# Attention stream cut into quarters, stages placed by quarter, layer norm applied on GpSimd

## The reference

```python
x = x + attn_a(layernorm(x))   # 16 heads share softmax(-|pos_i - pos_j| / 4), causal;
                               # pos = x @ w3d.T + b3d (3 numbers a token); values x @ wv.T + bv, then wo, bo
x = x + ffn(layernorm(x))      # sigmoid(xr @ W_r) * (relu(xk @ W_k)**2 @ W_v),
                               # xr, xk = mixtures of x and of x of the token before
x = x + attn_b(layernorm(x))   # 16 heads of 16: softmax(q.k / 4), causal, times v
x = x + ffn(layernorm(x))      # the same weights again
```

## Time and profile before

| | us |
|---|---|
| three runs | 2307.72, 2312.24, 2311.35 (median 2311.35) |
| profiled execution | 2312.75, span 2311.0, granted clock 0.888 |
| PE, DVE, ACT, POOL busy | 1933.2, 1502.9, 1234.3, 697.5 |
| first maximum of the stream | 195 us from the span's start |
| turns 1 to 7 end at | 452, 724, 1000, 1271, 1543, 1816, 2063 |

### The profile page before, as it was taken

The page is one execution under the profiler, slowest core; times in us unless marked ns, Lnnn a source line. Parts: engine busy times, 40 slices in busy tenths (PEclk is TensorE's granted clock), DMA queues, the critical chain, the costliest instruction groups (busy, mean ns, idle before and its releaser), DMA issues.

```text
span 2311.0 us, 32343 instructions
## 1 busy us (share of the span) xinstructions
PE 1933.2 (84%) x9842; PEld 977.6 (42%) x9842; DVE 1502.9 (65%) x4429; ACT 1234.3 (53%) x2673; POOL 697.5 (30%) x818
## 2 busy tenths in 40 slices
PE   5475888889888898888988888888988789898986
PEld 4343444444443444434444344434444344432433
DVE  3346677666676576766776567766767667787643
ACT  1632644755539454484546644485543945556563
POOL 2331242223323233233332233222332324322223
PEclk8787798979998899889998889988999889999998
DMA  3005013101231103211121112310122110231100
GB/s 96 0 31 106 1 29 83 19 10 29 65 83 28 28 7 87 56 29 28 38 83 28 29 29 65 83 29 1 29 74 73 29 28 20 71 67 29 29 20 19
DMA packets 64346, 97.26 MB, mean 42 GB/s; under 512 B 15655, under 2 KB 58029, under 8 KB 58030
## 3 DMA queue, kind: packets, MB, share of 16 engines
q1 hardware_dynamic: 64174, 95.20, 18.0%
HBM read 61.09 MB, written 33.55 MB: 41 GB/s over the span
## 4 chain that ended last, share of the span: by engine, by line
PE 62%; DVE 17%; ACT 10%; issue 7%; POOL 2%; DMA 1%; SPq 1%; DVEq 0%; POOLq 0%; ACTq 0%
PE o_bank L994 10%; PE max_bank L970 9%; PE side L879 9%; PE exp_bank L979 9%; PE side L835 6%; PE side L869 5%; PE side L921 4%; ACT pt L1030 4%; PE side L803 4%; DVE max_bank L1054 3%; ACT sq L479 3%; DVE st L243 3%; DVE xh L258 2%; PE side L815 2%; PE side L935 2%
## 5 line engine op out<-in xcount | busy, mean ns | idle before, releaser
L1030 ACT ACTIVATE pt<-exp_bank 128x512 f32<-128x512 f32 (+3 forms) x1536 | 685.9, 495 | 434.2 <-PE exp_bank L979 426.3
L1054 DVE CUSTOM_DVE_ANT_0 max_bank<-max_bank,mask 128x128 f32<-128x128 f32 (+3 forms) x1024 | 482.3, 514 | 221.6 <-PE max_bank L970 214.8
L979 PE MATMUL exp_bank<-qs,ks 98*128 98x512 bf16 (+3 forms) x1536 | 529.3, 355 | 68.0 <-ACT pt L1030 61.9
L970 PE MATMUL max_bank<-ks,qs 96*128 96x512 bf16 (+3 forms) x1536 | 528.8, 356 | 64.8 <-DVE piece_max L1054 38.9
L1058 DVE TENSOR_REDUCE piece_max<-max_bank 128x1 f32<-128x512 f32 x512 | 325.2, 684 | 93.5 <-PE max_bank L970 93.0
L994 PE MATMUL o_bank<-pt,v 128*17 128x512 f32 (+3 forms) x3072 | 356.7, 539 | 3.9 <-ACT ot L1040 2.3
L1106 POOL TENSOR_SCALAR_AFFINE_SELECT pt<-pt 128x512 f32<-128x512 f32 x256 | 174.9, 683 | 574.8 <-ACT pt L1030 574.6
L970 PEld LDWEIGHTS max_bank<-ks,qs 96*128 96x128 bf16 x1536 | 156.4, 103 | 366.9 <-DVE piece_max L1054 126.7
L979 PEld LDWEIGHTS exp_bank<-qs,ks 98*128 98x128 bf16 x1536 | 155.7, 102 | 292.2 <-ACT pt L1030 185.9
L803 PE MATMUL side<-ident,xh 128*128 128x128 f32 x512 | 109.3, 383 | 137.9 <-DVE xh L258 137.9
L458 ACT ACTIVATE xt<-side 128x512 f32<-128x512 f32 x128 | 74.6, 598 | 249.5 <-PE side L803 249.5
(11 more groups left out here) (93 smaller groups left out, 2231.8 us busy)
## 6 DMA issues: line engine op xcount, KB each, us to landing
parts_dram<-parts SPq DMA_DIRECT2D x64, 384.0 KB, 2.6
qs<-parts_dram SPq DMA_DIRECT2D x192, 128.0 KB, 6.5
ks<-parts_dram SPq DMA_DIRECT2D x32, 384.0 KB, 4.7
xs<-in_L_attn_a_x_dram SPq DMA_DIRECT2D x16, 512.0 KB, 4.5
ks<-parts_dram SPq DMA_DIRECT2D x32, 256.0 KB, 5.3
out_dram<-xs SPq DMA_DIRECT2D x16, 512.0 KB, 3.5
ks<-parts_dram SPq DMA_DIRECT2D x32, 128.0 KB, 5.7
qs<-neg_maxT SPq DMA_DIRECT2D x64, 8.0 KB, 1.8
```

The lines of the kernel that those rows point to most:

```text
L970: pe.matmul(max_bank[k % MAX_BANKS][:, 0:k1 - k0], qs[r][0:KROWS, j, P * tile:P * (tile + 1)], ks[r][0:KROWS, j, k0:k1], start=True, stop= ...
L979: pe.matmul(exp_bank[k % EXP_BANKS][:, 0:q1 - q0], ks[r][:, j, P * kt:P * (kt + 1)], qs[r][:, j, q0:q1], start=True, stop=True).then_inc(s ...
L1030: act.activation(pt[:, e % 2, j, 0:q1 - q0], exp_bank[k % EXP_BANKS][:, 0:q1 - q0], ACT.Exp, scale=SCALE).then_inc(exp_done, 1)
L1054: dve.tensor_tensor_reduce(max_bank[k % MAX_BANKS][:, 0:w], max_bank[k % MAX_BANKS][:, 0:w], mask[:, HALF - w:HALF], 1.0, LOWEST, ALU.add, ...
```

## The change

The tables `CHUNKS`, `TURNS` and `CHUNKS_AT` go. The unit of time is now a quarter, one head of a piece. `STAGES` gives each half of each stage a start in quarters, and `JOBS` gives every use of a side bank a line in its stage: name, number, first quarter, number of parts, quarters between them, quarters until the bank is emptied. `place` hands out the banks in order of use, puts each part of a job (two matmuls, or a set of transposes) into a quarter of its own, and moves a job to later when both banks are taken; `clock` moves the other engines' steps with them. In `schedule` every part is a generator that yields the quarter from which it may go on. The ffn's two halves start 16 quarters apart and overlap, `att1` of the next image starts inside `proj3`, and `ffn4` starts 32 quarters after `ffn2`. A full turn still has 192 quarters (48 pieces).

The layer norm is applied by POOL (`pool_normalise`), four instructions in quarters of their own, and the statistics have double buffers. The difference of neighbours goes to `xr` itself, `tm` no longer holds it. The stack for an image's first group is loaded at the end of `sp_proj3`. Nothing is added to or taken from the arithmetic.

```diff
-HALF_FFN = 11
-TAIL = 2 * (NS * (B - 1) + LEAD + (NG - 1) * NP + TPH + 3) + 1
-CHUNKS_AT = [0] * (2 * SLOTS)
...
+TURN = 4 * NS
+ATT1, FFN2, FFN4, PROJ3 = -44, 50, 82, 114
+FIRST = {("att1", 0): -220, ("ffn2", 0): -126, ("proj3", 0): -74,
+         ("att1", 1): -28, ("ffn2", 1): 66, ("proj3", 1): 114}
+OUTPUT_AT = [4 * (LEAD + TPH + 1) + 1, 4 * (LEAD + NP + 1) + 1]
+LN_HALF = {"att1": 8, "ffn2": 16, "ffn4": 16, "proj3": 12}
...
+PIECE_TIME = [2 + (q1 - q0) // P for _, q0, q1 in KEY_PIECES] + [5, 5, 5]
+PIECE_AT = [34 + sum(PIECE_TIME[:p]) for p in range(NP + 4)]
...
+JOBS = {"ln": [("tr", c, 12 + c, 1, 1, 2) for c in range(NC)],
+        "att1": [("values1", t, 16 + t + TPH * (t // TPH), 1, 1, 2) for t in range(NT)] +
+                [("positions", k, 29 + k, 1, 1, 1) for k in range(6)] +
+                [("attend", t, PIECE_AT[attended_from(t)] + 2, t // 2 + 1, 1, 2) for t in range(NT)],
+        "ffn": [("keys", j, 24 + 2 * j, 2, 1, 1) for j in range(2)] +
+               [("receptance", j, 31 + 2 * j, 2, 1, 1) for j in range(2)] +
+               [("products", j, 36 + 2 * j, 2, 1, 2) for j in range(2)],
+        "proj3": [("project", j, 24 + 3 * j, 2, 1, 1) for j in range(8)] +
+                 [("values3", j, 26 + 6 * j, 2, 3, 2) for j in range(4)]}
...
+    rows = [(4 * NP * (g + 1) + 1, ("maxima", g)) for g in range(GROUPS)]
+    rows += [(OUTPUT_AT[h] + 4 * NP * g + 5, ("output", g, h)) for g in range(GROUPS) for h in range(2)]
...
-            def apply(h):
-                q = q0 + h
-                dve.wait_ge(rstd_ready, q + 1)
-                if q > 0:
-                    dve.wait_ge(tr_full, 2 * q)
-                for t in range(TPH):
-                    last = dve.tensor_scalar(xh[:, t, :], src[:, TPH * h + t, :], mv[:, t, 0:1],
-                                             rstd[:, t:t + 1], ALU.subtract, ALU.mult)
-                last.then_inc(xh_ready, 1)
...
+        def pool_normalise(at, s, n, h):
+            pool, q = nc.gpsimd, LN_AT[s, n, h]
+            r, src = q % 2, xs[n % X_BUFFERS]
+            yield at(6)
+            pool.wait_ge(ln_step, 3 * q + 3)
+            pool.tensor_tensor(rstd[:, r, :], var_eps[:, r, :], minus_half[:, :], ALU.pow).then_inc(rstd_ready, 1)
+            pool.wait_ge(rstd_ready, q + 1)
+            if q > 0:
+                pool.wait_ge(tr_full, 2 * q)
+            for t in range(TPH):
+                yield at(7 + t)
+                pool.tensor_scalar(xh[:, t, :], src[:, TPH * h + t, :], mv[:, r, t, 0:1], rstd[:, r, t:t + 1],
+                                   ALU.subtract, ALU.mult).then_inc(xh_ready, 1)
...
-            for u in range(2 * SLOTS):
-                t, s = divmod(u, 2)
-                att(t, s)
-                rows(t, s)
-                for _ in range(CHUNKS_AT[u]):
-                    next(tail if u >= TAIL else chunks)
...
+            parts = [[next(part), part] for part in parts]
+            for u in range(BEGIN, END):
+                attention(u)
+                for entry in parts:
+                    while entry[0] <= u:
+                        entry[0] = next(entry[1], NEVER)
+                parts = [entry for entry in parts if entry[0] < NEVER]
```

More of the change, by code:

```diff
@@ L84 @@
-for k in range(HALF_FFN):
-    CHUNKS_AT[TAIL + (2 * SLOTS - TAIL) * k // HALF_FFN] += 1
+QUARTERS = 4 * SLOTS
+TURN = 4 * NS
[4 more added lines that the diff above has]
+LN_HALF = {"att1": 8, "ffn2": 16, "ffn4": 16, "proj3": 12}
+STAGES = []
+for n in range(B + 2):
+    if n < B:
+        STAGES += [(FIRST.get((s, n), TURN * (n - 1) + at), s, n, 0)
+                   for s, at in (("att1", ATT1), ("ffn2", FFN2), ("proj3", PROJ3))]
+    if 2 <= n <= B:
+        STAGES += [(TURN * (n - 1) + FFN4, "ffn4", n - 2, 0)]
@@ new lines, in stage_jobs, with place @@
+def stage_jobs(s, n, h):
+    jobs = [((name, s, n, h, k), *when) for name, k, *when in JOBS["ln"]]
+    body = "ffn" if s in ("ffn2", "ffn4") else s
+    if body == "ffn" or h == 0:
+        jobs += [((name, s, n, h, k), *when) for name, k, *when in JOBS[body]]
+    return jobs
+def place():
+    parts, delay = [], {}
+    for start, s, n, h in STAGES:
+        for key, first, count, step, after in stage_jobs(s, n, h):
+            delay[key] = after
+            parts += [(start + first + step * k, key, k, k == count - 1) for k in range(count)]
+    parts.sort(key=lambda part: part[0])
+    rows = [(4 * NP * (g + 1) + 1, ("maxima", g)) for g in range(GROUPS)]
+    rows += [(OUTPUT_AT[h] + 4 * NP * g + 5, ("output", g, h)) for g in range(GROUPS) for h in range(2)]
+    rows.sort()
+    quarters, bank, emptied, late = {}, {}, {}, []
+    free, before, shift, u = [BEGIN, BEGIN], BEGIN, 0, BEGIN
+    while parts or rows:
+        while rows and rows[0][0] <= u and min(free) <= u:
+            key = rows.pop(0)[1]
+            k = free.index(min(free))
+            quarters[key], bank[key], emptied[key] = [u], k, u + 2
+            free[k] = u + 2
+        if parts:
+            at, key, k, last = parts[0]
+            regained = max(0, shift - max(0, at - before) // 4)
+            if at + regained <= u and (k > 0 or min(free) <= u):
+                parts.pop(0)
+                before, shift = at, max(regained, u - at)
+                late.append((at, shift))
+                if k == 0:
+                    bank[key] = free.index(min(free))
+                    free[bank[key]] = NEVER
+                    quarters[key] = []
+                quarters[key].append(u)
+                if last:
+                    emptied[key] = free[bank[key]] = u + delay[key]
+        u += 1
+    return quarters, bank, emptied, late
@@ L87, with clock @@
+NEVER = 10 ** 6
+BEGIN = STAGES[0][0]
+PARTS_AT, BANK, EMPTIED_AT, LATE = place()
+BANK[0,], BANK[1,] = 0, 1
+END = max(EMPTIED_AT.values()) + 20
+WRITTEN_AT = {}
+for k in range(BEGIN, END):
+    since, shift = ([(BEGIN, 0)] + [entry for entry in LATE if entry[0] <= k])[-1]
+    WRITTEN_AT[k] = max(k + max(0, shift - (k - since) // 4), WRITTEN_AT.get(k - 1, BEGIN))
+def clock(start):
+    return lambda k: WRITTEN_AT[start + k]
 P1_AT = [sum(S - P * j for j in range(kt)) for kt in range(NT)]
@@ L587, in act_ffn @@
-            if half is not None:
-                yield
-        def act_proj3(n):
-            act = nc.scalar
-            yield
-            yield
-            act_transposed("proj3", n, 0)
-            yield
-            yield
-            act_transposed("proj3", n, 1)
-            yield
+            for j in range(2):
+                yield EMPTIED_AT["keys", s, n, h, j]
+                relu_k(j)
+            for j, k, late in ((0, 0, 0), (0, 1, 1), (1, 0, 0), (0, 2, 3), (1, 1, 2), (1, 2, 4)):
+                yield EMPTIED_AT["receptance", s, n, h, j] + late
+                sigmoid(j, k)
@@ new lines, in schedule @@
+        def schedule(attention, maxima, output, stage):
+            parts = [maxima(g) for g in range(GROUPS) if maxima]
+            parts += [output(g, h) for g in range(GROUPS) for h in range(2) if output]
+            parts += [part for start, s, n, h in STAGES for part in stage(clock(start), s, n, h)]
+            parts = [[next(part), part] for part in parts]
[5 more added lines that the diff above has]
+                parts = [entry for entry in parts if entry[0] < NEVER]
+            assert not parts
@@ L1189, in _ @@
                     sp_load(n, h)
[L1191 to L1200 removed]
+            schedule(sp_att3, sp_maxima, None, lambda at, s, n, h: [sp_proj3(at, n)] if s == "proj3" and h == 0 else [])
             for n in range(B - 2, B):
```

1122 lines of the change are left out of this document (432 added, 690 removed).

## The result

The changed kernel takes 2314.84 us (median of 20 runs, 2307.77 to 2319.97), the kernel before 2309.33 (median of 20 runs). The ratio of after to before is 1.0023, 95% interval 1.0014 to 1.0032: slower by 0.2%, where I had forecast 2109 us.

The account below looks back on a forecast made before the run. Full turns decide: PE needs 200 of 272.8 us, the rest being idle time, low clock and an unnamed part. Gains of 143 (five turns), 22, 34 and 3 make 202: 2311 - 202 = 2109 us, range 1990 to 2270.

Parts of the forecast that it names:

- the layer norm's wait: PE's wait before the layer norm's transposes, 15.6 us a full turn: 2 would stay, 13.6 be gained.
- the clock: PE's low clock in the full turns: 15 us a turn would return.
- my 27 us of lost clock: Full turns of the kernel before: up to 27 us a turn taken as lost to PE's low clock.
- What goes is the starving at eight layer norms a turn: Full turns: overlapping stages and smaller parts end PE's starving and the low clock there; 15 of 27 us return.
- The wait only moves: Rival, 4%: waits at side banks and the maxima's transposes (48 us) take back what the layer norm frees; about 2311 us.
- POOL's application: 0.45 us taken: One layer norm application instruction on POOL: 0.45 us assumed, bounded by 0.34 and 1.27.
- POOL's application comes too late: Rival, 10%: PE waits at each of 54 halves in turns 1 to 7 for a too long chain; 2397 us.
- Ahead of the stream: Before the first turn, 195 us: POOL's application costs little more, image 1's work fills a wait; 3 us gained.
- Turn 1: First turn, 257 us: 20 us of clock return with 13.6 of wait, 34 gained.
- turn 7: Seventh turn, 247 us: it has six of eight halves, so 22 us gained.
- The maxima's transposes: Transposes two quarters nearer their last maximum: 1.5 us in each of 32 groups, 48 us, could be lost; nothing taken.
- About 10 us that I cannot name: Part of the 73 us between a full turn's 272.8 us and PE's 200 us at full clock, left unexplained.

Follow-up runs that it names:

- early_emptying: The changed kernel with each side bank's emptying written one quarter after its last matmul, two before for some, refilling unmoved: 2182.9 us, 0.9449 of the kernel before.
- all_three: The changed kernel with every side bank emptied one quarter after its last matmul, DVE applying the layer norm ahead of the stream: 2120.7 us, 0.9169 of the kernel before.
- apply_on_dve: The changed kernel with the layer norm applied by DVE again, in the same quarters as by POOL: 2332.8 us, 1.0089 of the kernel before.

## Why the prediction was wrong

**The full turns: right removal, wrong remainder.** I predicted 13.6 us from the layer norm's wait and 15 from the clock. The wait for the application went altogether (15.6 of 15.6 us a turn), though PE still stands 5.3 us a turn before the same transposes, for banks. No row shows my 27 us of lost clock; what the trace of the kernel before shows is two levels: of the 2728 stretches of 0.5 us from 452 to 1816 us 2134 stand at 1.00, 523 at 0.50 and 71, in which it changes, between; L815's products start 0.43 us apart at 0.50 (44 to 47 us) and 0.22 apart at 1.00 (48 to 52 us). A mean of 0.90 is then 20% of a turn at the low level, 54 us that do the work of 27. In the changed kernel the clock rose to 0.94 (303 of 2734 stretches at 0.50); 12% of the time at the low level instead of 20% is some 11 us less lost by my own reckoning, where I said 15. But a full turn went from 273.0 to 273.2. The step that failed is "What goes is the starving at eight layer norms a turn" with nothing put in its place: the new waits for side banks, a term that I left at nothing. In the runs these and the other waits before side matmuls took 26 us a turn, where all but the application's had taken 7, so PE idles 38 us a turn and not the 22 that my sum came to (36 less 13.6). I gave the rival "The wait only moves" 4%, with side banks named in it, and argued its price from how busy DVE and ACT are. That was the wrong view, as busy shares say nothing of an emptying that is queued behind work which itself waits for PE. `early_emptying` shows the price: 20 us a full turn, 15 of them idle time of PE, and 132 in all. I had read `JOBS`, and had not asked which engine comes first within a quarter.

How the 11 us of the clock split is not settled: PE's busy time fell by only 1 us a turn, from 1182.7 to 1177.7 in five. Nor is it shown what sets the level: PE idled 36 us a turn at a clock of 0.90 and 38 at 0.94. Its float32 work now stands in parts, and fewer of their instructions overlap in the records, which alone makes busy time longer: L835's 94.7 us are 113.3 in L544, with 53 and 44 us of overlap (the sum of the lengths less the busy time), and L869's 81.0 are 90.3 in L644, with 20 and 13. I have no run that separates it.

**The forecast turn is nearly that of `all_three`.** I said 244 us and a clock of 0.95 or more; `all_three` has 246.9 and 0.96, and PE idles 21 us a turn there, where my sum came to 22. So the sizes of the wait and of the clock were about right, for a kernel in which most of the bank waits are gone. With early emptying of the stages' banks alone it is 253.3 and 0.94.

**POOL's application: 0.45 us taken, 1.27 measured.**

```profile
L353 POOL TENSOR_SCALAR xh<-xs,mv,rstd 128x256 f32<-128x256 f32 x256 | 322.6, 1266 | 10.0 <-PE side L379 3.8
```

I chose the value nearest in elements and inputs between 0.34 and 1.27; the upper bound, an addition of twice the size, was the truth. "No POOL row of this size is over 0.78" was no argument. On POOL it takes 1.27 us, where it took 0.45 on DVE in the kernel before. In the full turns PE never waits for it, because the room is 10.7 us (I had 10), and having it on POOL and not on DVE is worth 6 to 7 us a turn, where I had counted nothing. The rival "POOL's application comes too late" was right only where I hadn't placed it: ahead of the stream.

**Ahead of the stream: -3 predicted, +13.5 measured.** Nothing lies beside the chain there. PE's wait in the first 208 us:

```profile
PE side L379 <- POOL xh L353: 31.3, 5, 10.6
```

It is 26.0 us in the kernel before and 19.2 in `apply_on_dve`, both for DVE's `xh`. With DVE in those stages the stream starts 12 us earlier.

**Turn 1: -34 predicted, -23 measured; turn 7: -22, +6 measured.** Both hold the same bank waits (turn 1 is 216 and turn 7 237 us with early emptying, 41 and 10 less than before). **The rest:** 0 predicted, +4.

**The maxima's transposes:** 48 us held as a bound, nothing taken. L910 idles 10.4 us in five turns, all of it for a bank and none for the maxima. Taking nothing for DVE's small instructions was right.

**"About 10 us that I cannot name":** part stood in the earlier trace rows all along. L994 is busy 225.8 us in five turns, 45 a turn, where I put 37 from a single product at 384 columns. The distances stayed as they were: 0.84 and 62 of 75 us of ACT, 0.86 and 60.6 before. Two small sums are off and change nothing: the chain with 1.27 us each is 8.0 and not 8.1, and six quarters of 1.25 us are 7.5 and not 7.6.

## What to carry to other kernels

When two engines take turns on a buffer and one table says when each gets its instruction, ask within a slot who comes first: an emptying queued behind work that depends on the refilling engine's last step comes late, however idle the emptier is. Before giving a wait's removal its full price, list what the new order makes wait next, resource by resource, and price each. And put an operation that no row shows at its upper bound where nothing hides it, at the start above all.
